# First attention: the norm's last step on ScalarE, top values copied once per four tiles, expert weights rounded once out of a ring of raw chunks

## The chip, the cores and the metric

The kernel runs on one core of one Trainium2 chip. The metric is the device time of one execution in microseconds (us), lower is better. The kernel before was timed three times; a further execution was profiled.

## What is computed

Two transformer layers over 16 sequences of 256 tokens of width 256, each a cross attention over 77 context rows followed by a mixture of experts. Cut to the part that the change touches, the first layer:

```python
x = x + _L0_xattn_ref(_layernorm(x), ctx, ctx, ...)   # 16 heads of 16, query and key layernorm, softmax
x = x + _L0_ffn_ref(_layernorm(x), moe_router, moe_w13, moe_w2)
# inside the second:
router_logits = jnp.einsum('td,de->te', x_flat, moe_router)          # 8 experts
topk_logits, topk_idx = jax.lax.top_k(router_logits, 2)
w13_out = jax.lax.ragged_dot(x_sort, moe_w13, group_sizes)           # 8 x 256 x 1024 weights
```

The first attention phase ends each tile of 128 tokens with x1 = x + attention, xn = layernorm(x1), the eight router logits, and their sorted values and indices. In its idle time it also splits the 8 MB of expert weights w13 into a rounded high part, which stays in SBUF, and a low part, which goes to DRAM and is loaded again by the next phase.

## The kernel before

The program is a row of phases (projection, first attention, first routing, first experts, second attention, and so on), each a block that all engines leave together at a barrier. Within a phase every engine runs its own instruction list in order and waits on semaphores.

The change lies in `attention0_phase`. It handles 32 tiles of 128 tokens (`NT`), each in two halves of eight heads, so 64 halves u (`NU`). The function `half(u)` is written once for each engine and says what that engine does in half u. A stage with skew T works in half u on the tile with 2t = u - T. In half u TensorE does the scores of u (L777), the transposes of the probabilities of u-1 (L788) and the products with V of u-2 (L805); in even halves it adds the transposes L814 and L823 and the router product (L841), in odd ones the output projection (L833, T_WP = 7) and the transpose of xn (L852, T_X = 9). VectorE takes the maximum (L665) and subtracts it (L670) for every half; in odd halves it normalises the heads, writes x1 (L699) and takes its mean and variance; in even halves it waits for POOL's inverse root, applies the norm (L159, `ln.apply`) and sorts the eight logits of the tile with skew T_R = 10 (`top_of`, L477 to L485). ScalarE evicts PSUM (L730, L742, L749, L756) and does the exponentials (L735). POOL runs two halves ahead (`LEAD`): it spreads queries and keys (L623, L630, L636), adds the bias (L649) and computes the inverse root (L108, L110). Halves 16 to 63 are a hardware loop of eight halves; halves 0 to 15 and the tail, halves 64 to 74, are written out.

The weights: SP loads w13 into SBUF in eight pieces of 1 MB near the phase's start. They are handled as 64 chunks of 128 x 256 (`CHUNKS`), one for each half from u = 8. ScalarE writes the rounded chunk to `low` (L723, T_HIGH), POOL subtracts it from the raw chunk (L640, T_LOW), and two halves after the first step ScalarE stores `low` (L760) and rounds the chunk in place (L762, T_ROUND). There are four `low` buffers.

SP's list for a tile s is: load x of tile s, store x1 of tile s-4 (L602), store xn of tile s-4 (L604). In the next phase SP loads `pad_row` (L1254) and the low weights (L1257).

Of the kernel before, what the change touches and what calls it, by code (L numbers as in the profile page):

```python
# [6 lines left out]
F32 = mybir.dt.float32  # L7
F32R = mybir.dt.float32r
# [8 lines left out]
P = 128  # L17
# [95 lines left out]
class LayerNorm:  # L113
# [30 lines left out]
    def shift(self, pool, t):  # L144

        p = t.mod(self.ring)
        pool.wait_ge(self.s_rstd, t.n + 1)
        pool.tensor_scalar(self.less[p][:, :], self.mv[p][:, 0:1], self.rstd[p][:, :], -1.0, ALU.mult, ALU.mult)\
            .then_inc(self.s_less, 1)
# [327 lines left out]
def top_of(dve, g, scores, top, ix, t, s_scores, s_top, s_ix, passed):  # L477

    wait_alone(dve, s_scores, t.n + 1, passed[0])
    dve.max(top[:, :], scores[:, :]).then_inc(s_top, 1)  # L480
    wait_alone(dve, s_top, t.n + 1, passed[0])
    dve.max_index(ix[:, :], top[:, :], scores[:, :]).then_inc(s_ix, 1)
    dve.tensor_copy(g.top_v[:, bass.ds(t.n * 8, 8)], top[:, :])
    wait_alone(dve, s_ix, t.n + 1, passed[0])
    dve.tensor_copy(g.top_i[:, bass.ds(t.n * 8, 8)], ix[:, :])  # L485


def attention0_phase(nc, g):
# [3 lines left out]
    with ctx:  # L492
        def sb(name, shape, dt=F32):
# [4 lines left out]
        NU = NT * NG  # L498
        VW = H * (DH + 1)
# [21 lines left out]
        top = [sb(f"top{i}", [P, 8]) for i in range(2)]  # L521
        ix = [sb(f"ix{i}", [P, 8], U32) for i in range(2)]
        low = [sb(f"low{i}", [P, CHUNK], F32R) for i in range(4)]
        s_w, s_next, s_w13_first, s_w13, w_high, w_low, w_round = (sem(n) for n in (
            "s_w", "s_next", "s_w13_first", "s_w13", "w_high", "w_low", "w_round"))
        s_x, x1_st, xn_st = ([sem(f"{n}{i}") for i in range(2)] for n in ("s_x", "x1_st", "xn_st"))
        low_st = [sem(f"low_st{i}") for i in range(4)]
# [15 lines left out]
        T_RAW, T_N, T_O, T_WP, T_X, T_R = 4, 5, 6, 7, 9, 10  # L543
# [8 lines left out]
        T_HIGH, T_LOW, T_ROUND = 8, 9 + LEAD, 10  # L552

        W13_LATE = 3
# [10 lines left out]
        def _(sp):  # L565
# [3 lines left out]
            for dst, src in ((g.tri, g.ins["tri"]), (g.iota, g.ins["iota"]), (g.iota16, g.ins["iota16"]),  # L569
                             (g.not_first, g.ins["not_first"][:, 0:E0 * NT]), (g.tokval, g.ins["tokval0"])):  # L570
                sp.dma_start(dst[:, :], src).then_inc(s_next, 16)
# [8 lines left out]
            def expert_weights(e):  # L580
                n = DC * 2 * M0
                sp.dma_start(g.w13[:, e * n:(e + 1) * n], g.ins["w13"][:, e * n:(e + 1) * n])\
                    .then_inc(s_w13 if e else s_w13_first, 16)

            expert_weights(0)
            for t in range(2):
                input_rows(At(None, 0, t))
            for e in range(1, E0 - W13_LATE):
                expert_weights(e)

            def tile(s):
                t = s
                if t.within(NT):
                    if not (t.loop is None and t.off < 2):
                        input_rows(t)
                    if t.loop is None and 2 <= t.off < 2 + W13_LATE:
                        expert_weights(E0 - W13_LATE + t.off - 2)
                t = s.shift(-4)
                if t.within(NT):
# [4 lines left out]
                    sp.dma_start(g.xn[bass.ds(t.n * P, P), :], xn[p][:, :]).then_inc(xn_st[p], 16)  # L604

            steps(sp, 6, NT, NT + 4, 2, tile)
# [4 lines left out]
            for st in low_st:  # L611
                sp.wait_ge(st, CHUNKS // 4 * 16)

        @block.gpsimd
        def _(pool):
            def half(u):
# [21 lines left out]
                if i is not None:  # L638
                    pool.wait_ge(w_high, i.n + 1)
                    pool.tensor_tensor(low[i.mod(4)][:, :], chunk(i), low[i.mod(4)][:, :], ALU.subtract).then_inc(w_low, 1)  # L640
# [10 lines left out]
                if t is not None:  # L651
                    ln.invert(pool, t)

# [3 lines left out]
        def _(dve):  # L657
            dve.memset(ps_raw, 0.0).then_inc(ps_clear, 1)

            def half(u):  # L660
# [42 lines left out]
                if t is not None:  # L703
# [3 lines left out]
                    top_of(dve, g, lg[p], top[p], ix[p], t, lg_done, m8_done, ix_done, passed)  # L707
# [4 lines left out]
        def _(act):  # L712
            def half(u):
                i = chunk_at(u, T_HIGH)
                if i is not None:
                    if i.loop is None and i.off == 0:
                        act.wait_ge(s_w13_first, 16)
                    if i.loop is None and i.off == CHUNKS // E0 - 1:

                        act.wait_ge(s_w13, (E0 - 1) * 16)  # L720
# [1664 lines left out]
```

## Time and profile before

| | us |
|---|---|
| median of 3 timed runs | 1511.56 (1511.35 to 1512.79) |
| the profiled execution's own time | 1501.55 |
| its span, first to last instruction | 1499.7 |
| first attention phase in it | 110.6 to 373.5 |

The profiled execution took 10.0 us less than the median of the timed ones, and 1.85 us of its time lie outside its span. Times of the trace are microseconds from the span's start. Mean granted TensorE clock is 0.938 of full.

### The profile page before, as it was taken

The numbers are of one execution on the slowest core, as the hardware profiler recorded it, in microseconds if no ns is written. First come the engines' busy times: TensorE is split into PE (matmuls) and PEld (weight loads), VectorE is DVE, ScalarE is ACT, GpSimd is POOL, SyncE is SP. The second block draws the span as 40 slices with busy tenths as digits, with TensorE's granted clock in tenths as the row PEclk, the third lists the DMA queues.
The fourth block names the chain that finished last, engine by engine and source line by source line (L and its number), as shares of the span: only waits on it lengthen the run. The fifth ranks groups of instructions, "written<-read, shape, count | busy, mean of one in ns | idle before, by whom it ended". The sixth has DMA issues, their size and how long they took to land. (4 is left out here: it accounts for less than half of the span.)

```text
span 1499.7 us, 29032 instructions
## 1 busy us (share of the span) xinstructions
PE 1334.3 (89%) x7717; PEld 1055.5 (70%) x7718; DVE 766.2 (51%) x1962; ACT 585.5 (39%) x1311; POOL 654.1 (44%) x903
## 2 busy tenths in 40 slices
PE   7989999997979999999994998569999998577877
PEld 4656777775668888888883776258888885366655
DVE  4875888886822233223224886913333333154546
ACT  2555777775322222222222775533333332111110
POOL 1213656564023333333332763055555551655552
PEclk9998999998989999999996998579999999888989
DMA  2208222223721111111115885455555575333433
GB/s 92 63 29 326 91 88 84 87 79 112 281 95 50 52 52 49 49 52 52 49 39 172 260 227 178 174 182 156 158 164 164 161 141 124 103 112 106 122 115 99
DMA packets 117292, 179.69 MB, mean 120 GB/s; under 512 B 17178, under 2 KB 91947, under 8 KB 113900
## 3 DMA queue, kind: packets, MB, share of 16 engines
q1 hardware_dynamic: 80980, 100.29, 20.1%
q0 software_dynamic: 20640, 56.39, 14.2%
q10 hardware_dynamic: 15608, 22.25, 4.2%
q8 instruction: 29, 0.48, 0.1%
q14 instruction: 35, 0.29, 0.1%
HBM read 115.00 MB, written 59.64 MB: 116 GB/s over the span
## 5 line engine op out<-in xcount | busy, mean ns | idle before, releaser
L1228 POOL DMA_INDIRECT xg<-t_xn,token x160 | 151.3, 946 | 160.8 <-remote 61.7
L2168 POOL DMA_INDIRECT su_yg<-t_y,slot x128 | 123.2, 963 | 114.3 <-DVE su_acc L2197 44.5
L2106 PE MATMUL psum<-gu,m_xT 128*128 x640 | 153.4, 383 | 3.2 <-ACT m_xT L2037 3.2
L1465 PE MATMUL psum<-w,m_hT 128*128 x568 | 134.5, 380 | 0.8 <-ACT m_hT L1384 0.8
L1403 DVE TENSOR_TENSOR m_h<-psum,m_h 128x512 f32<-128x512 f32 x71 | 49.2, 692 | 162.7 <-ACT m_h L1378 88.9
L2106 PEld LDWEIGHTS psum<-gu,m_xT 128*128 128x128 f32 x640 | 116.5, 192 | 16.5 <-issue 3.7
L1444 PE MATMUL psum<-w,m_xT_high 128*128 x284 | 119.2, 420 | 0.0
L1444 PE MATMUL psum<-w,m_xT_low 128*128 x284 | 113.3, 399 | 0.0
L1444 PE MATMUL psum<-w_low,m_xT_high 128*128 x284 | 112.6, 396 | 0.0
L1465 PEld LDWEIGHTS psum<-w,m_hT 128*128 128x128 f32 x568 | 102.4, 190 | 12.2 <-issue 1.2
L1378 ACT ACTIVATE m_h<-psum 128x512 f32<-128x512 f32 x71 | 42.4, 597 | 151.7 <-PE psum L1444 151.7
L2073 DVE COPY m_y<-psum 128x512 f32<-128x512 f32 x80 | 54.9, 687 | 79.0 <-remote 37.0
L2065 DVE TENSOR_TENSOR m_h<-psum,m_sg 128x256 f32<-128x256 f32 x80 | 34.0, 425 | 119.0 <-ACT m_sg L2044 60.1
L1858 ACT ACTIVATE sh_sg<-psum 128x512 f32<-128x512 f32 x32 | 19.1, 598 | 193.3 <-PE psum L1837 75.7
L2037 ACT ACTIVATE m_xT<-psum 128x512 f32<-128x512 f32 x80 | 47.8, 598 | 108.6 <-remote 87.7
L777 PE MATMUL psum<-at_kblk,at_q_s 128*128 128x308 f32 x256 | 82.9, 448 | 7.3 <-DVE w L670 4.0
L730 ACT ACTIVATE at_prT<-psum 77x1024 f32<-77x1024 f32 x64 | 65.3, 1020 | 59.8 <-PE psum L788 59.8
L1384 ACT ACTIVATE m_hT<-psum 128x512 f32<-128x512 f32 x71 | 42.5, 599 | 112.4 <-PE psum L1465 112.4
L2127 PE MATMUL psum<-dn,m_hT 128*128 x320 | 84.0, 388 | 1.8 <-DVE m_y L2073 1.7
L1352 POOL DMA_INDIRECT t_y<-top_v,dest x36 | 35.5, 986 | 108.8 <-DVE top_v L1410 108.5
L1219 POOL DMA_INDIRECT xg<-t_xn,token x54 | 52.5, 973 | 68.4 <-POOLq L1237 48.4
L1352 POOL DMA_INDIRECT t_y<-top_i,dest x35 | 34.5, 987 | 106.2 <-DVE top_i L1410 100.7
(305 smaller groups left out, 3185.6 us busy)
## 6 DMA issues: line engine op xcount, KB each, us to landing
t_y<-m_y SPq DMA_DIRECT2D x80, 256.0 KB
w<-in_w SPq DMA_DIRECT2D x8, 1024.0 KB, 11.1
t_x<-at_x SPq DMA_DIRECT2D x64, 128.0 KB, 2.0
t_w_low<-at_low ACTq DMA_DIRECT2D x64, 128.0 KB, 1.7
w_low<-t_w_low SPq DMA_DIRECT2D x8, 1024.0 KB, 13.1
at_yg<-t_y SPq DMA_DIRECT2D x32, 256.0 KB, 3.5
gu<-in_gu ACTq DMA_DIRECT2D x8, 1024.0 KB, 11.8
w<-in_x SPq DMA_DIRECT2D x16, 256.0 KB, 2.7
```

Source lines behind the costliest of these rows:

```text
L730: act.activation(prT[p][0:LK, :].rearrange("p (a k) -> p a k", a=2), ps_tp[0:LK, :, :], ACT.Copy)\
L777: last = pe.matmul(ps_s[:, a, 0:HW], q_s[p][:, gr * P:(gr + 1) * P], kblk[b.mod(2)][:, (2 * gr + a) * HW:(2 * gr + a + 1) * HW], start=Tru ...
L1219: pool.indirect_dma_start(out=g.xg0[j % GB][:, :], out_offset=None, in_=g.xn, in_offset=bass.IndirectOffsetOnAxis(ap=g.token[:, j:j + 1], ...
L1228: pool.indirect_dma_start(out=g.xg1[j % GB][:, k * D:(k + 1) * D], out_offset=None, in_=g.xn4, in_offset=bass.IndirectOffsetOnAxis(ap=g.to ...
L1352: pool.indirect_dma_start(out=g.y0, out_offset=bass.IndirectOffsetOnAxis(ap=g.dest[:, j:j + 1], axis=0), in_=y[p][:, :], in_offset=None).t ...
L1403: dve.tensor_tensor(h[p][:, :], ps_gu[p][:, 1, :], h[p][:, :], ALU.mult).then_inc(h_done, 1)
L1444: last = pe.matmul(ps_gu[p][:, half, :], x[p][:, tile], w[:, at], start=(c == 0 and w is w13_high and x is xT_high), stop=(c == DC - 1 and ...
L1465: last = pe.matmul(ps_y[:, 0:D], hT[:, c * P:(c + 1) * P], g.w2[:, bass.ds(ex * (MC * D) + c * D, D)], start=(c == 0), stop=(c == MC - 1))
L2073: dve.tensor_copy(y[p][:, :], ps_y[p][:, :]).then_inc(y_out, 1)
L2106: last = pe.matmul(ps_gu[p][:, k * 2 * M1:(k + 1) * 2 * M1], xT[p][:, at:at + P], g.gu[:, bass.ds(ex[k] * (DC * 2 * M1) + c * 2 * M1, 2 * ...
L2127: last = pe.matmul(ps_y[p][:, k * D:(k + 1) * D], hT[j.mod(HELD)][:, k * P:(k + 1) * P], g.dn[:, bass.ds(ex[k] * D, D)], start=True, stop= ...
L2168: pool.indirect_dma_start(out=yg[p][k][:, :], out_offset=None, in_=g.y1, in_offset=bass.IndirectOffsetOnAxis(ap=g.slot[:, at:at + 1], axis ...
```

## The change

1. The last step of the norm moves from VectorE (`ln.apply`, half 2t+8, before x1 and the sort) to ScalarE (`ln.apply_scalar`, T_XA = 8, the last instruction of the half). For it POOL computes one more column, minus mean times inverse root (`ln.shift`), right behind the inverse root.
2. The sorted values and indices of four tiles are gathered in one buffer each (`RANKED`), and copied to `top_v` and `top_i` once for four tiles instead of once for each tile.
3. The raw weights no longer go straight into SBUF's w13. SP loads them chunk by chunk, 128 KB each, into a ring of eight buffers (the eighth is the table `not_first`, which the phase does not use). ScalarE rounds a chunk once, from the ring into w13; POOL subtracts w13 from the ring's buffer in place; SP stores it. ScalarE's second rounding and its 64 stores are gone.
4. SP's list for a tile s becomes: store x1 and xn of tile s-4, load x of tile s-1, load raw chunks 2s-6 and 2s-5, store low chunks 2s-12 and 2s-11. At the phase's end SP waits for the last store out of `not_first` and then loads that table.

```diff
     def shift(self, pool, t):
 
         p = t.mod(self.ring)
-        pool.wait_ge(self.s_rstd, t.n + 1)
+        wait_alone(pool, self.s_rstd, t.n + 1, self.s_passed[1])
         pool.tensor_scalar(self.less[p][:, :], self.mv[p][:, 0:1], self.rstd[p][:, :], -1.0, ALU.mult, ALU.mult)\
             .then_inc(self.s_less, 1)
...
-def top_of(dve, g, scores, top, ix, t, s_scores, s_top, s_ix, passed):
+def top_of(dve, scores, top, ix, t, s_scores, s_top, s_ix, passed):
 
     wait_alone(dve, s_scores, t.n + 1, passed[0])
-    dve.max(top[:, :], scores[:, :]).then_inc(s_top, 1)
+    dve.max(top, scores[:, :]).then_inc(s_top, 1)
     wait_alone(dve, s_top, t.n + 1, passed[0])
-    dve.max_index(ix[:, :], top[:, :], scores[:, :]).then_inc(s_ix, 1)
-    dve.tensor_copy(g.top_v[:, bass.ds(t.n * 8, 8)], top[:, :])
-    wait_alone(dve, s_ix, t.n + 1, passed[0])
-    dve.tensor_copy(g.top_i[:, bass.ds(t.n * 8, 8)], ix[:, :])
...
-        low = [sb(f"low{i}", [P, CHUNK], F32R) for i in range(4)]
+        RING = 8
+        low = [sb(f"low{i}", [P, CHUNK], F32R) for i in range(RING - 1)] + [g.not_first[:, :].bitcast(F32R)]
+        low_st, s_raw = ([sem(f"{n}{i}") for i in range(RING)] for n in ("low_st", "s_raw"))
...
+            def weights(i):
+
+                p = i.mod(RING)
+                wait(sp, low_st[p], i.div(RING).n * 16)
+                sp.dma_start(low[p][:, :].bitcast(F32), g.ins["w13"][:, bass.ds(i.n * CHUNK, CHUNK)]).then_inc(s_raw[p], 16)
+
+            def weights_low(i):
+                p = i.mod(RING)
+                sp.wait_ge(w_low, i.n + 1)
+                sp.dma_start(g.w13_low_d[:, bass.ds(i.n * CHUNK, CHUNK)], low[p][:, :].bitcast(F32)).then_inc(low_st[p], 16)
+
             for t in range(2):
                 input_rows(At(None, 0, t))
-            for e in range(1, E0 - W13_LATE):
-                expert_weights(e)
+
+            W13_FROM, W13_LOW = 3, 6
...
             def tile(s):
-                t = s
-                if t.within(NT):
-                    if not (t.loop is None and t.off < 2):
-                        input_rows(t)
-                    if t.loop is None and 2 <= t.off < 2 + W13_LATE:
-                        expert_weights(E0 - W13_LATE + t.off - 2)
                 t = s.shift(-4)
                 if t.within(NT):
                     p = t.mod(2)
@@ -602,14 +596,27 @@
                     sp.dma_start(g.x1[bass.ds(t.n * P, P), :], x1[p][:, :]).then_inc(x1_st[p], 16)
                     sp.wait_ge(x_norm, t.n + 1)
                     sp.dma_start(g.xn[bass.ds(t.n * P, P), :], xn[p][:, :]).then_inc(xn_st[p], 16)
-
-            steps(sp, 6, NT, NT + 4, 2, tile)
+                t = s.shift(-1)
+                if t.within(NT) and not (t.loop is None and t.off < 2):
+                    input_rows(t)
+                t = s.shift(-W13_FROM)
+                if t.within(CHUNKS // 2):
+                    for i in range(2):
+                        weights(t.times(2).shift(i))
+                t = s.shift(-W13_LOW)
+                if t.within(CHUNKS // 2):
+                    for i in range(2):
+                        weights_low(t.times(2).shift(i))
+
+            steps(sp, 8, NT, NT + W13_LOW, 4, tile)
+            sp.wait_ge(low_st[RING - 1], CHUNKS // RING * 16)
+            sp.dma_start(g.not_first[:, :], g.ins["not_first"][:, 0:E0 * NT]).then_inc(s_next, 16)
...
                     pool.wait_ge(w_high, i.n + 1)
-                    pool.tensor_tensor(low[i.mod(4)][:, :], chunk(i), low[i.mod(4)][:, :], ALU.subtract).then_inc(w_low, 1)
+                    p = i.mod(RING)
+                    pool.tensor_tensor(low[p][:, :], low[p][:, :].bitcast(F32), chunk(i), ALU.subtract)\
+                        .then_inc(w_low, 1)
...
+                    ln.shift(pool, t)
...
-                t = tile_at(u, T_WP + 1)
-                if t is not None:
-                    p = t.mod(2)
-
-                    wait(dve, xn_st[p], t.div(2).n * 16)
-                    wait(dve, x_t, t.shift(-1).n)
-                    ln.apply(dve, x1[p][:, :], xn[p][:, :], t).then_inc(x_norm, 1)
...
-                    top_of(dve, g, lg[p], top[p], ix[p], t, lg_done, m8_done, ix_done, passed)
+                    at = slice(t.mod(RANKED) * 8, (t.mod(RANKED) + 1) * 8)
+                    top_of(dve, lg[p], top[:, at], ix[:, at], t, lg_done, m8_done, ix_done, passed)
+                    if t.mod(RANKED) == RANKED - 1:
+                        at = bass.ds(t.shift(1 - RANKED).n * 8, RANKED * 8)
+                        dve.tensor_copy(g.top_v[:, at], top[:, :])
+                        wait_alone(dve, ix_done, t.n + 1, passed[0])
+                        dve.tensor_copy(g.top_i[:, at], ix[:, :])
...
-                    wait(act, low_st[i.mod(4)], i.div(4).n * 16)
-                    act.activation(low[i.mod(4)][:, :], chunk(i), ACT.Copy).then_inc(w_high, 1)
+                    act.wait_ge(s_raw[i.mod(RING)], (i.div(RING).n + 1) * 16)
+                    act.activation(chunk(i).bitcast(F32R), low[i.mod(RING)][:, :].bitcast(F32), ACT.Copy).then_inc(w_high, 1)
...
-                i = chunk_at(u, T_ROUND)
-                if i is not None:
-                    act.wait_ge(w_low, i.n + 1)
-                    act.dma_start(g.w13_low_d[:, bass.ds(i.n * CHUNK, CHUNK)], low[i.mod(4)][:, :].bitcast(F32))\
-                        .then_inc(low_st[i.mod(4)], 16)
-                    act.activation(chunk(i).bitcast(F32R), chunk(i), ACT.Copy).then_inc(w_round, 1)
+                t = tile_at(u, T_XA)
+                if t is not None:
+                    p = t.mod(2)
+
+                    wait(act, xn_st[p], t.div(2).n * 16)
+                    wait(act, x_t, t.shift(-1).n)
+                    ln.apply_scalar(act, x1[p][:, :], xn[p][:, :], t).then_inc(x_norm, 1)
```

Two places show what this does to the order. The first is ScalarE's list in the tail, from half 64 on, after the loop. Before (`w` is w13, or scratch space in the spare of w2 in L742's case):

```order
L723 ACTIVATE at_low<-w 128x256
L730 ACTIVATE at_prT<-psum 77x1024
L749 ACTIVATE at_oT<-psum 128x256
L760 DMA t_w_low<-at_low 128x256
L762 ACTIVATE w<-w 128x256
L723 ACTIVATE at_low<-w 128x256
L742 ACTIVATE w<-psum 128x512
L756 ACTIVATE at_xnT<-psum 128x256
L760 DMA t_w_low<-at_low 128x256
L762 ACTIVATE w<-w 128x256
L723 ACTIVATE at_low<-w 128x256
L749 ACTIVATE at_oT<-psum 128x256
```

The same halves 64, 65 and the start of 66 of the changed kernel:

```order
L726 ACTIVATE w<-at_low 128x256
L733 ACTIVATE at_prT<-psum 77x1024
L752 ACTIVATE at_oT<-psum 128x256
L154 ACTIVATE at_xn<-at_x,at_ln_less,at_ln_rstd 128x256
L726 ACTIVATE w<-at_low 128x256
L745 ACTIVATE w<-psum 128x512
L759 ACTIVATE at_xnT<-psum 128x256
L726 ACTIVATE w<-at_low 128x256
L752 ACTIVATE at_oT<-psum 128x256
L154 ACTIVATE at_xn<-at_x,at_ln_less,at_ln_rstd 128x256
```

L760 and L762 are gone, the norm L154 stands last in each even half, and the first instruction of every half (L726) now reads a ring buffer that a DMA fills. The second place is SP's list at the end of the phase. Before, the stores of x1 and xn of the last three tiles and the branch out of the block:

```order
L602 DMA t_x<-at_x 128x256
L604 DMA t_xn<-at_xn 128x256
L602 DMA t_x<-at_x 128x256
L604 DMA t_xn<-at_xn 128x256
L602 DMA t_x<-at_x 128x256
L604 DMA t_xn<-at_xn 128x256
L492 UNCONDITIONAL_BRANCH
```

The same end in the changed kernel:

```order
L596 DMA t_x<-at_x 128x256
L598 DMA t_xn<-at_xn 128x256
L579 DMA at_low<-in_w 128x256
L579 DMA not_first<-in_w 128x256
L584 DMA t_w_low<-at_low 128x256 x2
L596 DMA t_x<-at_x 128x256
L598 DMA t_xn<-at_xn 128x256
L584 DMA t_w_low<-at_low 128x256 x5
L584 DMA t_w_low<-not_first 128x256
L613 DMA not_first<-in_not_first 128x256
```

Behind the last xn store stand six stores of low chunks, and the load of the table, which waits for the last of them.

## Rows read from the trace of the kernel before

**Rows 1.** Engine time in two stretches: PE, PEld, DVE, ACT, POOL busy, clock, DMA.

```profile
150.00:250.00 100.00, 100.00 (x968) 79.56 (x962) 86.55 (x215) 75.56 (x148) 63.98 (x104) 1.00 0.27 88
350.00:377.00 27.00, 17.65 (x123) 12.99 (x116) 16.93 (x65) 13.53 (x33) 10.89 (x19) 0.71 0.37 124
```

**Rows 2.** Timeline, TensorE: a half's first scores product, every eighth half; start, duration.

```profile
222.65 0.68 PE L777 MATMUL psum<-at_kblk,at_q_s 128*128 128x308 f32 x2
...
252.56 0.69 PE L777 MATMUL psum<-at_kblk,at_q_s 128*128 128x308 f32 x2
...
284.23 1.20 PE L777 MATMUL psum<-at_kblk,at_q_s 128*128 128x308 f32 x4
...
314.14 1.20 PE L777 MATMUL psum<-at_kblk,at_q_s 128*128 128x308 f32 x4
```

**Rows 3.** Timeline, VectorE and POOL, at the slow half and 30 us before.

```profile
227.62 0.16 DVE L485 COPY top_i<-at_ix 128x8 uint32 x1
...
257.54 0.40 POOL L636 COPY w<-kv 77x272 f32 x1
...
257.54 2.49 DVE L485 COPY top_i<-at_ix 128x8 uint32 x1
...
259.28 0.72 POOL L640 TENSOR_TENSOR at_low<-w,at_low 128x256 fp32r<-128x256 f32 x1
...
259.95 0.79 DVE L665 TENSOR_REDUCE at_mx<-psum 128x8 f32<-128x616 f32 x1
...
261.62 0.82 PEld L777 LDWEIGHTS psum<-at_kblk,at_q_s 128*128 128x128 f32 x4 [1.66 <-DVE w L670]
```

**Rows 4.** Groups by line inside the phase: busy us, mean ns of one | idle before.

```profile
L159 DVE TENSOR_SCALAR at_xn<-at_x,at_ln_mv,at_ln_rstd 128x256 f32<-128x256 f32 x27 | 26.2, 969 | 0.0
...
L762 ACT ACTIVATE w<-w (+1 forms) x64 | 26.6, 415 | 0.6 <-issue 0.2
...
L108 POOL TENSOR_SCALAR at_ln_rstd<-at_ln_mv 128x1 f32<-128x1 f32 x13 | 2.9, 221 | 36.7 <-DVE at_ln_mv L137 36.7
```

**Rows 5.** DMA issues by line, 150 to 350 us: KB each, median us to landing.

```profile
t_w_low<-at_low ACTq DMA_DIRECT2D x53, 128.0 KB, 1.7
at_x_in<-in_x SPq DMA_DIRECT2D x27, 128.0 KB, 2.1
```

**Rows 6.** Timeline, ScalarE in the steady part.

```profile
340.52 0.42 ACT L762 ACTIVATE w<-w  x1
...
344.42 0.38 ACT L756 ACTIVATE at_xnT<-psum 128x256 f32<-128x256 f32 x1
```

**Rows 7.** Timeline of the phase's end, all engines.

```profile
359.09 0.70 DVE L159 TENSOR_SCALAR at_xn<-at_x,at_ln_mv,at_ln_rstd 128x256 f32<-128x256 f32 x1 [1.21 <-POOL at_ln_rstd L110]
...
362.95 0.38 ACT L749 ACTIVATE at_oT<-psum 128x256 f32<-128x256 f32 x1 [1.38 <-PE psum L823]
...
363.42 2.05 PE L833 MATMUL psum<-at_wp,at_oT 128*128 128x256 f32 x4
...
366.22 0.42 DVE L699 TENSOR_TENSOR at_x<-psum,at_xb 128x256 f32<-128x256 f32 x1
...
368.65 0.70 DVE L159 TENSOR_SCALAR at_xn<-at_x,at_ln_mv,at_ln_rstd 128x256 f32<-128x256 f32 x1 [1.21 <-POOL at_ln_rstd L110]
...
369.37 0.33 SPq L604 DMA_DIRECT2D t_xn<-at_xn  x1
...
371.16 0.43 ACTq L760 DMA_DIRECT2D t_w_low<-at_low  x1
...
372.77 0.17 DVE L485 COPY top_i<-at_ix 128x8 uint32<-128x8 uint32 x1
...
373.47 0.35 SPq L1254 DMA_DIRECT2D r_pad_row<-in_pad_row  x1
...
373.87 4.12 SPq L1257 DMA_DIRECT2D w_low<-t_w_low  x8
```

More of the change, by code:

```diff
@@ L474, in _ @@
             steps(pe, FIRST, LAST, TOTAL, BODY, step)
-def top_of(dve, g, scores, top, ix, t, s_scores, s_top, s_ix, passed):
+def top_of(dve, scores, top, ix, t, s_scores, s_top, s_ix, passed):
     wait_alone(dve, s_scores, t.n + 1, passed[0])
-    dve.max(top[:, :], scores[:, :]).then_inc(s_top, 1)
+    dve.max(top, scores[:, :]).then_inc(s_top, 1)
     wait_alone(dve, s_top, t.n + 1, passed[0])
-    dve.max_index(ix[:, :], top[:, :], scores[:, :]).then_inc(s_ix, 1)
-    dve.tensor_copy(g.top_v[:, bass.ds(t.n * 8, 8)], top[:, :])
-    wait_alone(dve, s_ix, t.n + 1, passed[0])
-    dve.tensor_copy(g.top_i[:, bass.ds(t.n * 8, 8)], ix[:, :])
+    dve.max_index(ix, top, scores[:, :]).then_inc(s_ix, 1)
 def attention0_phase(nc, g):
@@ L498, in attention0_phase @@
         NU = NT * NG
+        RANKED = 4
         VW = H * (DH + 1)
@@ L520, in attention0_phase @@
         lg = [sb(f"lg{i}", [P, E0]) for i in range(2)]
-        top = [sb(f"top{i}", [P, 8]) for i in range(2)]
-        ix = [sb(f"ix{i}", [P, 8], U32) for i in range(2)]
-        low = [sb(f"low{i}", [P, CHUNK], F32R) for i in range(4)]
-        s_w, s_next, s_w13_first, s_w13, w_high, w_low, w_round = (sem(n) for n in (
-            "s_w", "s_next", "s_w13_first", "s_w13", "w_high", "w_low", "w_round"))
+        top, ix = sb("top", [P, RANKED * 8]), sb("ix", [P, RANKED * 8], U32)
+        RING = 8
+        low = [sb(f"low{i}", [P, CHUNK], F32R) for i in range(RING - 1)] + [g.not_first[:, :].bitcast(F32R)]
+        s_w, s_next, w_high, w_low = (sem(n) for n in ("s_w", "s_next", "w_high", "w_low"))
         s_x, x1_st, xn_st = ([sem(f"{n}{i}") for i in range(2)] for n in ("s_x", "x1_st", "xn_st"))
-        low_st = [sem(f"low_st{i}") for i in range(4)]
+        low_st, s_raw = ([sem(f"{n}{i}") for i in range(RING)] for n in ("low_st", "s_raw"))
         v_ready = sem("v_ready")
@@ L541, in attention0_phase @@
         block = ctx.enter_context(nc.Block())
-        T_RAW, T_N, T_O, T_WP, T_X, T_R = 4, 5, 6, 7, 9, 10
+        T_RAW, T_N, T_O, T_WP, T_XA, T_X, T_R = 4, 5, 6, 7, 8, 9, 10
         FIRST, BODY, TOTAL = 16, 8, NU + T_R + 1
@@ L550, in tile_at @@
             return s.div(2) if s.mod(2) == 0 and s.within(NU) else None
-        T_HIGH, T_LOW, T_ROUND = 8, 9 + LEAD, 10
-        W13_LATE = 3
+        T_HIGH, T_LOW = 8, 9 + LEAD
         def chunk_at(u, skew):
@@ L569, in _ @@
             for dst, src in ((g.tri, g.ins["tri"]), (g.iota, g.ins["iota"]), (g.iota16, g.ins["iota16"]),
-                             (g.not_first, g.ins["not_first"][:, 0:E0 * NT]), (g.tokval, g.ins["tokval0"])):
+                             (g.tokval, g.ins["tokval0"])):
                 sp.dma_start(dst[:, :], src).then_inc(s_next, 16)
@@ L611, in _ @@
             for st in low_st:
-                sp.wait_ge(st, CHUNKS // 4 * 16)
+                sp.wait_ge(st, CHUNKS // RING * 16)
         @block.gpsimd
@@ L715, in half @@
                 if i is not None:
[L716 to L720, printed above, removed]
-                    wait(act, low_st[i.mod(4)], i.div(4).n * 16)
-                    act.activation(low[i.mod(4)][:, :], chunk(i), ACT.Copy).then_inc(w_high, 1)
+                    act.wait_ge(s_raw[i.mod(RING)], (i.div(RING).n + 1) * 16)
+                    act.activation(chunk(i).bitcast(F32R), low[i.mod(RING)][:, :].bitcast(F32), ACT.Copy).then_inc(w_high, 1)
                 v = u.shift(-1)
```

5 lines of the change are left out of this document (removed).

## The prediction

> **What bounds the kernel now.** I first asked for the engines' busy time in stretches of the first attention phase [rows 1]. The columns are the stretch, its length, then busy time of matmuls, weight loads, VectorE, ScalarE and POOL, the clock, the DMA share and GB/s. In the steady part TensorE is busy all of 100 us, VectorE 86.6, ScalarE 75.6, POOL 64.0. A busy matmul row alone does not prove a bound, so I looked for a rhythm. The first scores product of a half, taken every eighth half, starts at 222.65, 252.56, 284.23 and 314.14 [rows 2]. The distances are 29.91, 31.67 and 29.91 us: eight halves cost 29.91 us, or 3.74 each, and one stretch of eight costs 1.76 more. Such a constant step, beside VectorE work whose instructions vary in length, says that TensorE's own list sets the pace, and VectorE only where it falls far behind.
>
> The one slow half shows how far [rows 3]. VectorE's copy of the indices (L485) starts at 257.54, at the very time at which POOL starts L636, and lasts 2.49 us, to 260.03. POOL's last instruction of that unbroken run, L640, ends at 259.28 + 0.72 = 260.00. The maximum of the next half starts only then, and TensorE's weight load for the scores finds nothing to do for 1.66 us. The same copy 30 us earlier took 0.16 us. So the copy lost a race for something it shares with POOL, and it waited for the whole run of POOL's instructions.
>
> The third stretch is the tail, from 350 us on: TensorE is busy 17.7 of 27 us, the clock is at 0.71 in the mean, and chains of small steps over all engines decide [rows 1, 7].
>
> **The change, part by part.**
>
> *VectorE loses the norm.* 969 ns for each tile, 26.2 us over 27 tiles [rows 4]. Since TensorE is the bound, this is worth nothing in the steady part. What it could free is the slack that the 2.49 us copy used up. It also loses three of four pairs of copies; those in a slow half are what matters. The remaining pair comes for tile t with t mod 4 = 3, in halves with u mod 8 = 0. The slow half was 38 (counting the maxima), that is u mod 8 = 6, and a long POOL run with the key spreading is there in every half with u mod 4 = 2. So the remaining copies fall outside of it. I take the whole 1.76 us as gain: **-1.76**. Bounds: 0, if a remaining copy meets such a run, and -1.76, for there was one.
>
> The Trainium skill (SBUF — State Buffer, Who interferes with whom) says that such a VectorE copy and a POOL instruction take a port pair as an exclusive lock for one whole instruction, and the loser blocks. By that rule the copy would have waited 0.40 us for L636, TensorE would have lost nothing, and the term would be 0. The row shows a wait through four instructions, and the sum goes by the row.
>
> *ScalarE.* It loses 64 roundings of 415 ns [rows 4] and 64 DMA issues, and gains 32 norms over the same 128 x 256 elements; I take 0.41 us from L762, its nearest row. Two thirds of a rounding's room are left over; the norm takes the place of L762 at 340.52 in the even half [rows 6]. Cost in the steady part 0, hidden by TensorE.
>
> *POOL* gains a one column instruction for each tile, 0.22 us as L108 [rows 4], about 0.35 with its wait. POOL is at 64% and, with work for two halves ahead, has the room. 0 in the steady part, 0.35 in the tail's last tile.
>
> *The raw chunks.* The first instruction of each ScalarE half now waits for a DMA. SP issues it behind the xn store of tile s-4, which waits for the new norm in half 2s; the chunk is wanted in half 2s+2. In the steady part: norm ends 341.03 (in L762's place, 340.52, with the time of L749 before it unchanged), 0.25 us for the semaphore, then the xn store, the x load and the first chunk load at about 0.45 each, so issue at 342.2, landing 2.1 us later [rows 5] at 344.3. ScalarE is free for it after L756, 344.42 + 0.38 = 344.80 [rows 6]. Half a microsecond is left, and behind it nearly a microsecond before the next eviction and about one more before TensorE misses the exponentials. So 0 here. The DMA traffic near the phase's start gets lighter (8 MB are no longer fetched at once), but nothing on the path waits for it.
>
> *In the tail* the halves are short on work and the room is gone. Before, tile 29's norm started at 359.09 and ended 359.79, ScalarE evicted tile 31's heads (L749) at 362.95, and the projection L833 started at 363.42 at the low clock level (2.05 us) [rows 7]. Now norm 29 ends at about 360.0 (POOL's extra column, ScalarE 0.41 instead of VectorE 0.70), the xn store and the load of chunk 60 are issued at 360.3 and 360.6, and the chunk lands at 362.7. ScalarE's rounding of it stands ahead of L749: 362.9 to 363.3, L749 to 363.65, L833 from 363.85, 0.4 later than before. It ends at 365.9, so x1 of tile 31 starts at 366.2, as before (366.22). VectorE would have been ready long before, since it no longer waits for POOL and has no norm: its gain in the tail is given back to the chunk's DMA. From x1 to the norm's start were 2.43 us (366.22 to 368.65); with 0.45 more for the column and ScalarE 0.41 the norm of tile 31 ends at 366.2 + 2.43 + 0.45 + 0.41 = 369.5. VectorE's end after it would be some 0.4 us later than 372.94 was.
>
> *SP's end* is what counts. Before, the last low chunk was stored by ScalarE at 371.16 and landed 1.7 us later, at 372.9, when VectorE's last copy ended also (372.77 + 0.17); the next phase began at 373.47 [rows 5, 7]. Now SP issues the xn store at 369.7 and behind it six stores. Eight issues in a row took 4.12 us, 0.515 each [rows 7], so the sixth store starts at 369.7 + 0.38 + 5 x 0.515 = 372.65 and lands at 374.35. Only then is the table's load issued, 0.2 us later; it lands after 2.1 us [rows 5] at 376.65. With the 0.4 to 0.5 us of the barrier the next phase begins at about 377.1: **+3.6**. Bounds: -0.4 if the DMA chain overlapped better than I read it and VectorE's end, earlier by the unhindered norm, decided; +5.5 if each of the two DMAs takes a microsecond more.
>
> *The sum:* -1.76 + 3.6 = +1.84 us. Against the profiled execution's own 1501.55 us that is 1503.4. It is 0.12% of the time, and I carry it over to the median unchanged: 1511.56 + 1.84 = **1513.4 us**. A measurement of this kernel can tell about 0.2%, 3.0 us, from no change, so the forecast is no change that can be told.
>
> **The rivals.**
>
> *More copies lose the race in the timed runs (faster).* The timed runs took 10.0 us more than the profiled one. If that were such stalls, there would be 10.0 / 1.76 = 5.7 more of them; sixteen tiles have the copy near POOL's long run. The change would remove them all: 1511.56 - 10.0 - 1.76 + 3.6 = 1503.4. For it speaks that the race of rows 3 was decided within 0.01 us. Against it, that the three runs lie within 1.4 us, and that the rest of the difference may be clock or launch. It is faster by over 3.0 us from three more stalls on.
>
> *The tail does not grow (no change, or barely faster).* If SP's last store lands while VectorE still sorts, only the table's load, or nothing, is added: 1511.56 - 1.76 - 0.4 = 1509.4 up to 1511.6. It stays within 0.2%.
>
> *A chunk that comes late in the steady part (slower).* The place is ScalarE's first instruction in each even half. TensorE starts to wait when a chunk lands more than 2.1 + 0.5 + 0.95 + 0.9 = about 4.5 us after its issue. Seven transfers of 128 KB for each tile are now in one queue, where two queues shared five. Each 0.5 us beyond that point would be paid in some 26 tiles: 13 us, or 1511.56 + 1.84 + 13 = 1526.4. The median of 2.1 us speaks against it.
>
> *The tail grows more (slower).* If both last DMAs take the upper bound, +5.5 - 1.76 = 3.7: 1515.3.
>
> *The change does nothing:* with the one stall returning somewhere else, +3.6: 1515.2, also just over 0.2%.
>
> **How the numbers follow.** My forecast with its own spread (1509.5 to 1514.5) and the rival of a tail that doesn't grow are both within 0.2%: 0.45 and 0.10. More stalls in the timed runs: 0.22. Late chunks 0.10; a tail over 5 us or a stall elsewhere 0.13. So faster 0.22, same 0.55, slower 0.23. The range leaves out about one in ten on each side: below, the greater part of the stall case reaches to 1505.5; above, it takes in the long tail and the mildest late chunks, to 1517.
>
> **What would show it.** Right: the steps of eight halves all at 29.91 us; L726 never waits for a DMA in the loop, but does in halves 66 and 68 of the tail; six low stores in a row behind the last xn store, and the next phase's first instruction about 4 us after VectorE's last copy (0.5 before). Wrong: a step of eight halves below 29.9 would mean that TensorE was not the bound; waits of L726 in the loop that show on TensorE; a copy of 128 x 32 of over 2 us; or later phases that change with an unchanged instruction list, as by the clock.

## The result and the profile after

The changed kernel took 1515.19 us in the median of 20 timed runs, the kernel before 1511.02 us beside it (20 runs; the three known ahead gave 1511.56). The ratio is 1.0032, with a 95% interval of 1.0016 to 1.0048: slower by 2.4 to 7.3 us. The forecast was 1513.4 us and "no change that can be told". The time fell inside the range and 1.8 us from the forecast. But 4.2 us are more than the 3.0 us (0.2%) that the forecast took as its limit, and the interval excludes 1, so by that limit the outcome is "slower". One run of the changed kernel (4607.62 us) and one each of E3, E4 and E8 below (1519.06, 2270.01 and 5546.67 us) count as slow runs, which stand in the medians but not in the ratios.

The profiled execution of the changed kernel took 1512.32 us, 10.8 us more than that of before. Most of that difference is not the change. The timed runs of the kernel before lie 15 to 22 us apart in each comparison, and the profile of before was among its shortest. So whole times are compared by timed runs only, and what the change does is read where it acts, between three marks that every trace has: TensorE's first weight load for the scores (the phase's start), its last such group (half 63, end of the steady part), and SP's `pad_row` load (the next phase's start). In the changed kernel these are, from the timelines of weight loads and of SP:

```profile
113.79 0.50 PEld L781 LDWEIGHTS psum<-at_kblk,at_q_s 128*128 128x128 f32 x2 [3.23 <-POOL at_kblk L637]
...
346.58 0.82 PEld L781 LDWEIGHTS psum<-at_kblk,at_q_s 128*128 128x128 f32 x4
...
375.81 0.34 SPq L1258 DMA_DIRECT2D r_pad_row<-in_pad_row  x1
```

Before, the same marks stood at 112.26, 347.67 and 373.47. So the part up to half 63 went from 235.41 to 232.79 us, and the tail from 25.80 to 29.23. The phase grew by 0.81 us. Of the first part's 2.62 us, 1.74 are the lost slow half (halves 11 to 63 took 196.18 and now 194.44). The other 0.88 lie in the third half of the phase, which took 3.97 us before and 3.09 now; that comes and goes with the clock. The granted clock was 0.50 from 120 to 122 us before, and 1.00 throughout the same half of the changed kernel. The three profiles of the kernel before (the first, and E9 and E12 below) have 3.97, 3.09 and 3.94 us there.

The steady rhythm is TensorE's, as [rows 2]. The matmul timeline of the changed kernel shows two of its steps, read at the second of a half's four products:

```profile
219.82 0.94 PE L781 MATMUL psum<-at_kblk,at_q_s 128*128 128x308 f32 x3
...
249.73 0.94 PE L781 MATMUL psum<-at_kblk,at_q_s 128*128 128x308 f32 x3
...
279.65 0.94 PE L781 MATMUL psum<-at_kblk,at_q_s 128*128 128x308 f32 x3
```

29.91 and 29.92 us for eight halves, with no slow one. VectorE's load fell and TensorE's pace did not move. The engines' time from 150 to 350 us says it once more (columns as in [rows 1]; before, VectorE had 173.51 us here and ScalarE 149.09):

```profile
150.00:350.00 200.00, 200.00 (x1935) 159.03 (x1934) 146.48 (x360) 146.40 (x267) 129.46 (x227) 1.00 0.38 120
```

VectorE gave up 27 us of work. ScalarE came out nearly even, since its norm costs more than I took. The groups by line in the same stretch:

```profile
L726 ACT ACTIVATE w<-at_low 128x256 f32 (+1 forms) x46 | 18.9, 411 | 3.0 <-DMA at_low<-in_w 2.2
L154 ACT ACTIVATE at_xn<-at_x,at_ln_less,at_ln_rstd 128x256 f32<-128x256 f32 x27 | 16.0, 591 | 0.0
```

The norm takes 591 ns, a plain copy of the same shape 411. The first row shows also that the raw chunks are nearly late in the loop: five waits of over 0.15 us, 2.2 us in all and 0.80 the longest, one before the loop and four in it. None of them reaches TensorE, which waits for no other engine in this stretch.

The tail is where the time went. ScalarE's timeline there:

```profile
357.82 0.42 ACT L726 ACTIVATE w<-at_low 128x256 fp32r<-128x256 f32 x1 [2.26 <-DMA at_low<-in_w]
358.14 0.37 ACT L752 ACTIVATE at_oT<-psum 128x256 f32<-128x256 f32 x1
...
362.01 0.42 ACT L726 ACTIVATE w<-at_low 128x256 fp32r<-128x256 f32 x1 [1.69 <-DMA at_low<-in_w]
362.34 0.36 ACT L752 ACTIVATE at_oT<-psum 128x256 f32<-128x256 f32 x1
...
367.17 0.60 ACT L154 ACTIVATE at_xn<-at_x,at_ln_less,at_ln_rstd 128x256 f32<-128x256 f32 x1 [0.94 <-POOL at_ln_less L148]
```

In halves 66 and 68 ScalarE waits 2.26 and 1.69 us for a raw chunk (0.72 more in half 70), and the eviction L752, on which TensorE's projection depends, stands behind it. SP's timeline at the end, which answers to the lower part of [rows 7]:

```profile
367.79 0.33 SPq L598 DMA_DIRECT2D t_xn<-at_xn  x1
368.17 2.42 SPq L584 DMA_DIRECT2D t_w_low<-at_low  x5
370.63 0.45 SPq L584 DMA_DIRECT2D t_w_low<-not_first  x1
372.48 0.34 SPq L613 DMA_DIRECT2D not_first<-in_not_first  x1
375.81 0.34 SPq L1258 DMA_DIRECT2D r_pad_row<-in_pad_row  x1
```

Six stores, a wait until the last has landed, the table's load, a wait for that, and the barrier. VectorE's last copy had ended at 371.23, so 4.6 us before the next phase; before it was 0.5.

### The profile page after: what moved, and what is told of

Read it like the earlier page. It is cut to its first block and busy times, and to the rows that moved or that the text cites. A ratio compares the mean times of both kernels' runs of the same rounds, so it can differ in the third digit from the quotient of the medians.

```text
span 1510.5 us, 29130 instructions
## 1 busy us (share of the span) xinstructions
PE 1329.5 (88%) x7717; PEld 1051.3 (70%) x7718; DVE 736.4 (49%) x1882; ACT 582.8 (39%) x1279; POOL 661.9 (44%) x935
```

## The experiments

Each profile is read by the same marks. "Halves 11 to 63" is taken between TensorE's weight loads of these two halves. The columns for the whole time compare timed runs with those of the kernel before on the same chip. The ratio is estimated from the single runs and is not the quotient of the two medians: for E2 that would be 1.0047, for E3 1.0018.

| kernel | halves 11 to 63 | tail | phase | median / before beside it | ratio (95%) |
|---|---|---|---|---|---|
| before | 196.18 | 25.80 | 261.21 | | |
| changed | 194.44 | 29.23 | 262.02 | 1515.19 / 1511.02 | 1.0032 (1.0016 to 1.0048) |
| E1 ring alone | 196.20 | 29.83 | 264.38 | 1510.55 / 1505.66 | 1.0023 (0.9988 to 1.0057) |
| E2 norm alone | 200.70 | 23.43 | 263.09 | 1512.78 / 1505.66 | 1.0063 (1.0031 to 1.0094) |
| E3 copies alone | 194.44 | 24.86 | 257.65 | 1508.44 / 1505.66 | 0.9998 (0.9967 to 1.0028) |
| E4 before, table late | 194.44 | 28.32 | 261.87 | 1509.28 / 1505.66 | 1.0014 (0.9984 to 1.0044) |
| E5 table first | 194.44 | 27.17 | 259.96 | 1508.19 / 1506.44 | 1.0022 (0.9998 to 1.0045) |
| E6 chunks ahead | 194.44 | 26.46 | 259.82 | 1508.77 / 1506.44 | 1.0018 (0.9995 to 1.0042) |
| E7 E5 and E6 | 194.44 | 23.62 | 256.41 | 1507.51 / 1506.44 | 1.0007 (0.9978 to 1.0036) |
| E8 changed, again | 194.44 | 29.12 | 261.91 | 1510.02 / 1508.52 | 1.0020 (1.0000 to 1.0041) |
| E9 before, again | 194.44 | 25.80 | 258.58 | 1502.17 / 1508.52 | 0.9969 (0.9946 to 0.9993) |
| E10 E7, norm on VectorE | 194.44 | 25.24 | 258.73 | 1506.95 / 1508.52 | 0.9991 (0.9966 to 1.0016) |
| E11 E7, again | 194.43 | 23.66 | 257.37 | 1506.33 / 1505.56 | 1.0012 (0.9987 to 1.0037) |
| E12 before, third | 194.44 | 25.80 | 259.43 | 1505.48 / 1505.56 | 1.0005 (0.9980 to 1.0030) |

**E1: the ring alone.** Items 3 and 4 of the change; the norm stays on VectorE, the copies stay one for each tile. Against the changed kernel:

```diff
+                t = tile_at(u, T_WP + 1)
...
+                    ln.apply(dve, x1[p][:, :], xn[p][:, :], t).then_inc(x_norm, 1)
...
+                    top_of(dve, g, lg[p], top[p], ix[p], t, lg_done, m8_done, ix_done, passed)
...
-                t = tile_at(u, T_XA)
...
-                    ln.apply_scalar(act, x1[p][:, :], xn[p][:, :], t).then_inc(x_norm, 1)
```

> Only the ring of raw chunks with SP's loads and stores; norm and top copies as before. Theory A (the cost is SP's list at the phase's end, and the raw chunk that ScalarE waits for in the tail): the tail, from TensorE's last first-of-half weight load of the scores to SP's pad_row load, is 28.5 to 30 us (before 25.80, after 29.23), the steady part is 29.91 us per eight halves, and the time is 2 to 4 us longer than before's. Rival B (the cost came with the norm on ScalarE): the tail is within 0.7 us of 25.8 and the time within noise of before's.

The tail is 29.83 us, 4.0 more than before. The ring alone carries the tail's whole cost. By the ratio the kernel is 3.5 us slower, as expected, though the interval holds 1. The steady part, which I had expected at 29.91 for every eight halves, had the slow half again, in the same place. The timelines of VectorE, POOL and TensorE's weight loads there:

```profile
256.61 2.49 DVE L485 COPY top_i<-at_ix 128x8 uint32 x1
...
256.61 0.40 POOL L647 COPY w<-kv 77x272 f32 x1
...
260.69 0.82 PEld L778 LDWEIGHTS psum<-at_kblk,at_q_s 128*128 128x128 f32 x4 [1.66 <-DVE w L683]
```

**E2: the norm alone**, item 1 only, last in ScalarE's half behind the second rounding, which stays, as do the four low buffers and ScalarE's stores. Against the kernel before:

```diff
-                t = tile_at(u, T_WP + 1)
...
-                    ln.apply(dve, x1[p][:, :], xn[p][:, :], t).then_inc(x_norm, 1)
...
+                t = tile_at(u, T_WP + 1)
...
+                    ln.apply_scalar(act, x1[p][:, :], xn[p][:, :], t).then_inc(x_norm, 1)
```

> Only the norm on ScalarE (with POOL's extra column); four low buffers, ScalarE's second rounding and stores as before. Theory A: the tail stays at 25.8 us within 1, steady part 29.91 per eight halves, the time within 2 us of before's; a slow half by a lost copy can still appear. Rival B: the tail grows by 2 us or more, and the time by as much.

Both expectations missed. The tail is not 25.8 but 23.43, and the steady part is 6.3 us longer than an undisturbed one. The kernel is slower by 0.63% (0.31 to 0.94), 4.7 to 14.2 us; its phase is longer than that of E9 and E12 (the kernel before, below) by 4.5 and 3.7 us, which accounts for the lower end of that.

In fourteen places of the steady part a half took 3.80 to 3.97 us instead of at most 3.76, some 2.1 us in all. Twelve of them lie four halves apart: they are the halves in which VectorE's copies meet POOL's spreading of the keys. The timelines of VectorE, POOL and TensorE's weight loads at one of them:

```profile
198.03 1.08 DVE L485 COPY top_i<-at_ix 128x8 uint32 x1
...
196.68 2.40 POOL L630 TENSOR_TENSOR at_kblk<-kv,hmask 128x616 f32<-128x616 f32 x2
...
199.84 0.80 DVE L671 TENSOR_TENSOR w<-psum,at_mx 128x616 f32<-128x616 f32 x1
...
200.70 0.82 PEld L778 LDWEIGHTS psum<-at_kblk,at_q_s 128*128 128x128 f32 x4 [0.18 <-DVE w L671]
```

The copy ends when POOL's spreading ends (196.68 + 2.40 = 199.08). Without the norm ahead of it VectorE's sort comes earlier, and its copies fall under that instruction. VectorE's subtraction L671 is then late, and TensorE waits for it. ScalarE is also short of room: before its next eviction it is idle for 0.49 us in the mean (23.0 us over 47 waits), where the changed kernel has 0.94 (49.6 us over 53). But no wait of TensorE for ScalarE is recorded in this stretch. The other 4.1 us are two halves in a row of 6.23 and 5.39 us, behind a value copy of 1.23 us and an index copy of 2.49 right after each other on VectorE. So item 1 by itself costs time in the steady part, and what the trace shows of it are copies that wait for POOL. The changed kernel has a quarter of these copies, through item 2, and in other halves: its value copy took 0.60 to 0.72 us in six of them, and TensorE never waited. No run separates whether ScalarE's second rounding has a share in E2's loss.

**E3: the copies alone**, item 2, against the kernel before.

```diff
-                    top_of(dve, g, lg[p], top[p], ix[p], t, lg_done, m8_done, ix_done, passed)
...
+                    top_of(dve, lg[p], top[:, at], ix[:, at], t, lg_done, m8_done, ix_done, passed)
+                    if t.mod(RANKED) == RANKED - 1:
...
+                        dve.tensor_copy(g.top_v[:, at], top[:, :])
...
+                        dve.tensor_copy(g.top_i[:, at], ix[:, :])
```

> Only the sorted values and indices copied once per four tiles. If the 1.76 us stall before was one of several per timed run, the time drops by 2 us or more; if it is a rare event, the time is before's within noise (2 us) and the tail is 25.8 within 0.7 us. No copy of over 2 us in either case.

No slow half, a tail of 24.86 us (0.24 outside of what I gave it), and a whole time that can't be told from before's: 0.9998. The interval's lower end, 0.9967, is 5.0 us, so a saving of the 5.7 stalls of 1.76 us that the rival asked for is excluded; one or two stalls for each timed run are not.

**E4: the kernel before with only the table's load moved to the end.**

```diff
-                             (g.not_first, g.ins["not_first"][:, 0:E0 * NT]), (g.tokval, g.ins["tokval0"])):
+                             (g.tokval, g.ins["tokval0"])):
...
             steps(sp, 6, NT, NT + 4, 2, tile)
+            sp.wait_ge(low_st[3], CHUNKS // 4 * 16)
+            sp.dma_start(g.not_first[:, :], g.ins["not_first"][:, 0:E0 * NT]).then_inc(s_next, 16)
```

> The kernel before, with the load of not_first alone moved to the phase's end, behind the landing of the last low chunk. Theory A: SP's pad_row load comes 2.1 to 2.6 us later, so the tail is 28.0 to 28.5 us, and the time is about 2.3 us (0.15%) longer. Rival: the barrier already waits on something else, and the tail stays at 25.8.

The tail grew by 2.52 us, as theory A has it. SP's timeline:

```profile
371.15 0.35 SPq L608 DMA_DIRECT2D not_first<-in_not_first  x1
...
374.15 0.35 SPq L1256 DMA_DIRECT2D r_pad_row<-in_pad_row  x1
```

From the load's issue to the next phase 3.0 us. This run has every instruction of the loop as before, and no slow half.

**E5: the table as the ring's first buffer**, so that the last low chunk in it is chunk 56 and not chunk 63, and its load ahead of the last xn store.

```diff
-        low = [sb(...) for i in range(RING - 1)] + [g.not_first[:, :].bitcast(F32R)]
+        low = [sb(...) for i in range(RING - 1)]
+        low = [g.not_first[:, :].bitcast(F32R)] + low
...
+                    if s.loop is None and s.off == NT + 3:
+                        sp.wait_ge(low_st[0], CHUNKS // RING * 16)
+                        sp.dma_start(g.not_first[:, :], ...)
                     sp.wait_ge(x_norm, t.n + 1)
...
-            sp.wait_ge(low_st[RING - 1], CHUNKS // RING * 16)
-            sp.dma_start(g.not_first[:, :], ...)
```

> The changed kernel, with the table not_first as the ring's first buffer instead of its last, so that it is free two tiles earlier, and its load ahead of the last xn store. Theory A (two separate costs in the tail: the table's load behind the last store, and the late raw chunks): the tail falls by the load's 2.3 to 2.9 us, from 29.23 to between 26.3 and 27.0 us; ScalarE's waits for raw chunks stay at about 2.3, 1.7 and 0.7 us. Rival (the stores alone fill the queue and the load was hidden behind them): the tail stays above 28.5.

The tail is 27.17 us, 2.06 less than the changed kernel's, slightly short of the 2.3 expected. ScalarE's waits for chunks stayed (2.48, 1.40 and 0.42 us). SP's timeline, with the load out of the chain:

```profile
365.31 0.34 SPq L600 DMA_DIRECT2D not_first<-in_not_first  x1
366.76 0.33 SPq L602 DMA_DIRECT2D t_xn<-at_xn  x1
367.13 2.90 SPq L585 DMA_DIRECT2D t_w_low<-at_low  x6
372.20 0.34 SPq L1260 DMA_DIRECT2D r_pad_row<-in_pad_row  x1
```

**E6: raw loads and low stores ahead of SP's wait for xn.**

```diff
                     sp.dma_start(g.x1[bass.ds(t.n * P, P), :], x1[p][:, :]).then_inc(x1_st[p], 16)
-                    sp.wait_ge(x_norm, t.n + 1)
-                    sp.dma_start(g.xn[bass.ds(t.n * P, P), :], xn[p][:, :]).then_inc(xn_st[p], 16)
-                t = s.shift(-1)
-                if t.within(NT) and not (t.loop is None and t.off < 2):
-                    input_rows(t)
                 t = s.shift(-W13_FROM)
...
                         weights_low(t.times(2).shift(i))
+                t = s.shift(-4)
+                if t.within(NT):
+                    p = t.mod(2)
+                    sp.wait_ge(x_norm, t.n + 1)
+                    sp.dma_start(g.xn[bass.ds(t.n * P, P), :], xn[p][:, :]).then_inc(xn_st[p], 16)
+                t = s.shift(-1)
+                if t.within(NT) and not (t.loop is None and t.off < 2):
+                    input_rows(t)
```

> The changed kernel, with SP's loads of raw chunks and stores of low chunks put ahead of its wait for xn, the table's load still last. Theory A: ScalarE's waits for raw chunks in the tail are gone (under 0.3 us each), two stores fewer stand behind the last xn store, and the tail falls to between 26 and 27.5 us; the steady part stays at 29.91 per eight halves. Rival (the raw chunk was not what held ScalarE): only the two stores count, 1.0 us, and the tail is 28 us or more.

As theory A has it: 26.46 us, and no wait of ScalarE for a chunk in the tail. The waits of ScalarE from 346 us on are now for POOL's column and for TensorE:

```profile
ACT at_xn L154 <- POOL at_ln_less L148: 3.6, 3, 1.4
ACT at_xnT L762 <- PE psum L859: 1.5, 4, 0.5
```

The same view of the changed kernel:

```profile
ACT w L726 <- DMA at_low<-in_w: 4.7, 3, 2.3
ACT at_xnT L759 <- PE psum L856: 2.2, 4, 1.2
```

**E7: both.**

> Both mendings. Theory A: the costs add, the tail is 23 to 24.5 us, less than before's 25.8, because ScalarE's norm no longer holds VectorE up there; the phase from the first scores to the next phase is 256 to 258 us (before 261.2 with one stall and 259.4 without, after 262.0), and the time is 1 to 4 us shorter than before's. Rival: something else comes up behind them (POOL's subtractions), and the tail stays above 25 us.

The tail is 23.62 us, 5.61 less than the changed kernel's; E5 and E6 alone took off 2.06 and 2.77. The savings add, with 0.8 to spare. The tail is also 2.2 us shorter than before's 25.80: with the ring's two costs gone, the norm on ScalarE and the fewer copies do shorten it. SP's timeline:

```profile
365.79 0.33 SPq L613 DMA_DIRECT2D t_xn<-at_xn  x1
366.17 1.91 SPq L585 DMA_DIRECT2D t_w_low<-at_low  x4
370.24 0.34 SPq L1263 DMA_DIRECT2D r_pad_row<-in_pad_row  x1
```

Within the phase this kernel beats both: 256.41 us. In the whole time it does not show: 1.0007 (0.9978 to 1.0036), where I had expected it 1 to 4 us below before's.

**E8 and E9: the changed kernel and the kernel before once more,** unaltered.

> The changed kernel once more, unaltered. Theory A (the change acts in the first attention phase alone): steady part 194.4 us with no slow half, tail 29.0 to 29.5 us, phase 262 us; the rest of the span, from the next phase on, between 1126 and 1141 us like every other kernel's, no matter which. Rival C (the change also makes later phases longer): the rest is again longer than that of the kernel before run beside it by 3 us or more.

> The kernel before once more, unaltered, to see how often its slow half comes and how long the rest of its span is when profiled again. Theory A: tail 25.8 us within 0.3; steady part 194.4 or 196.2 us, as one copy wins or loses its race; the rest of the span 1130 to 1141 us, well above the 1126.2 of the first profile, which was one of the fastest runs. Rival C: the rest is again below 1129 us.

The marks repeat to 0.1 us: tails of 29.12 and 25.80. E9 has no slow half. The same copy and the same POOL instruction in E9, to be held against E1's above and [rows 3]:

```profile
256.57 0.17 DVE L485 COPY top_i<-at_ix 128x8 uint32 x1
...
256.58 0.43 POOL L636 COPY w<-kv 77x272 f32 x1
...
258.96 0.82 PEld L777 LDWEIGHTS psum<-at_kblk,at_q_s 128*128 128x128 f32 x4
```

Here the copy took 0.17 us; in E1 and in the first profile, at the same place, it took 2.49. The printed starts do not tell the two cases apart. In E12 (below) both stand at the same hundredth, as in E1, and the copy is short:

```profile
257.43 0.17 DVE L485 COPY top_i<-at_ix 128x8 uint32 x1
...
257.43 0.43 POOL L636 COPY w<-kv 77x272 f32 x1
```

The rows ahead of the meeting, in the first profile, say why the two start together:

```profile
257.23 0.39 DVE L483 COPY top_v<-at_top 128x8 f32 x1
...
256.33 1.26 POOL L630 TENSOR_TENSOR at_kblk<-kv,hmask 128x616 f32<-128x616 f32 x1
```

VectorE's value copy took 0.39 us instead of 0.17 and ended at 257.62, when POOL's spreading had ended (257.59). Both engines go on from there, within the same hundredth. This happens in every fourth half, thirteen times in the steady part of each profile of the kernel before.

From the next phase to the span's end ("the rest") E8 took 1500.1 - 374.20 = 1125.9 us and E9 1498.1 - 370.75 = 1127.35; the first two profiles had 1134.7 (changed) and 1126.2 (before). For E9 I had said 1130 to 1141, and under 1129 for rival C: there the rival's mark came true, and it did in E12 too (1128.1). Against rival C stands E8, the changed kernel with the shortest rest of all. Of the eleven profiles that are not of the kernel before, nine have 1130.4 to 1140.6 us, and only E8 and E11 (1126.7) less. So the rest alone does not settle it. Where the difference lies says more. From `pad_row` to the first instruction of the second attention phase, which takes in the first routing and the first experts, all fourteen profiles took 428.2 to 429.3 us (before 428.9 to 429.3, changed 429.1 and 429.2). The spread arises later, and with identical kernels: the last phase, to the span's end, took 245.3 us in E7 and 230.4 in E11. E9's whole time was 0.31% below that of the same program beside it, with an interval that excludes 1.

**E10: E7 with the norm back on VectorE.**

> Both mendings of the tail, with the norm back on VectorE and POOL's extra column gone; top copies per four tiles and the ring stay. If the norm on ScalarE is what made the tail shorter than before's, the tail grows from 23.62 to between 24.5 and 26 us (copies per four tiles alone had 24.86); if the norm's place is worth nothing, the tail stays within 0.5 us of 23.6. Steady part 194.4 us either way.

The tail is 25.24 us, 1.62 more than E7's, inside the first expectation. That is what the norm on ScalarE is worth, and only in the tail.

**E11 and E12: E7 and the kernel before once more.**

> The twice mended kernel once more, unaltered. Theory A: phase from first scores to next phase 256.4 us within 1, that is 2.2 us less than an undisturbed before (258.6) and 5.5 less than the changed kernel (261.9); the whole time differs from before's by less than the comparison can tell (ratio 0.996 to 1.001). Rival: the whole time is again above before's by over 0.1%, which would speak for a cost of the change outside of this phase.

> The kernel before a third time, unaltered, beside its own timed runs: what the comparison shows when nothing is changed. If the last such ratio, 0.9969 (0.9946 to 0.9993), was chance or the load of that program, this one lies anywhere between 0.996 and 1.004. Tail 25.8 us; steady part 194.4 or 196.2 us.

E11's phase is 257.37 us, its ramp 0.9 us longer than E7's with the clock; its ratio of 1.0012 lies 0.0002 over what I had given it and just past the 0.1% that I had named for the rival, a cost outside of this phase. Its interval (0.9987 to 1.0037) holds 1, but not the gain of 2.2 us (0.9985) that its phase would give. E12 gives 1.0005 with nothing changed. E9 and E12 together say that a ratio of 0.3% can come from loading the same program again.

## Why the forecast came out as it did

**TensorE is the bound of the steady part: right.** Halves 11 to 63 took 194.43 or 194.44 us in eleven of fourteen profiles, with VectorE's work in this stretch changed by 27 us. Taking the norm off VectorE was worth nothing there.

**The stall of 1.76 us: right in mechanism, wrong as a term.** I took the whole of it as gain, "for there was one". Of the five profiles that keep the copy for each tile and the norm on VectorE (before, E1, E4, E9, E12), two have it, both at the same place. In each of the five the index copy and POOL's instruction start within 0.01 us of each other thirteen times: 65 meetings, of which the copy lost two. The eight profiles with a copy for four tiles have no such stall. So what the change saves is about 2/5 of 1.75, or 0.7 us for a run, with five profiles as all there is for the share. This is the step that failed: the saving was sized at its full height where it should have been an expectation over runs. With 0.7 in place of 1.76 the sum is +2.9 and the forecast 1514.5. The rival with 5.7 more stalls in the timed runs fell with E3.

**ScalarE and POOL in the steady part at no cost: right together, though mis-sized.** The norm took 0.59 us instead of 0.41. Alone it does cost: E2 lost 2.1 us over fourteen halves and 4.1 in a long stall, both behind VectorE copies that waited for POOL. I had not seen that the sort moves under POOL's long instruction once the norm ahead of it is gone; in the changed kernel, with item 2, it does not show. (By its own rows ScalarE had a whole rounding's room left in each tile, 0.42 us, not two thirds of one.) POOL's column took 265 ns with 0.21 us of wait ahead of it, where I had 0.35 in all.

**The raw chunks in the loop: right in cost, wrong in the sign to look for.** I had said that ScalarE never waits for one in the loop, with half a microsecond of room and a landing time of 2.1 (the norm's end in that sum should read 340.93 by its rows, not 341.03); the loads took 2.4 in the median and ScalarE waited 2.2 us in all. TensorE lost nothing.

**The tail: right, +3.43 measured for +3.6, though two misses cancel in it.** The tail began 1.09 us earlier than before's (346.58 for 347.67), and that is taken off in what follows. The eviction behind the late chunk came at 362.34 (I said about 363.3; 0.1 later). Then I was too slow: the projection behind it took 1.50 us and not 2.05, for the granted clock was 0.67 in the mean from 362 to 366 us, where before's stood at 0.50 from 362.5 to 366.5. So x1 of tile 31 started at 364.29 (366.2; 0.8 earlier) and the sixth store at 370.63 (372.65; 0.9 earlier):

```profile
362.75 1.50 PE L837 MATMUL psum<-at_wp,at_oT 128*128 128x256 f32 x4 [1.70 <-ACT at_oT L752]
...
364.29 0.42 DVE L702 TENSOR_TENSOR at_x<-psum,at_xb 128x256 f32<-128x256 f32 x1 [2.32 <-PE psum L837]
```

Behind the stores I was too fast: from the table's load to the next phase it took 3.33 us, where I had 2.55. The next phase began at 375.81 (377.1; 0.2 earlier). E5 and E6 take the two costs away one by one, and E4 puts one of them into the kernel before. E7 shows that +3.4 is a net sum: the ring's order costs 5.6 us, and the norm and the copies give back 2.2, where I had the gain in the tail at nothing.

**The sign.** Outside the ramp, an undisturbed before takes 194.44 + 25.80 = 220.24 us and the changed kernel 223.67, so +3.4; over runs with the stall's share +2.7. The timed medians say +4.2, with 2.4 to 7.3 us as interval. The phase accounts for the lower part of that; E9 shows that the rest can be chance of the measurement. I found nothing outside the phase that the change made longer, and the two phases behind it are unchanged within 1.1 us. But E7 and E11, whose phase is shorter than before's, are not faster as a whole either. Whether there is a cost of a few us in later phases stays open. The range's upper side and the chance of 0.23 for slower held this outcome; as the likeliest one I had a change that cannot be told.

## What to carry to other kernels

When an engine with slack is relieved, look for what the relief costs at the phase's end. In a loop of 7.5 us for each tile seven transfers in one queue were free; in the tail, where a tile takes 4 us, a load issued behind the previous tile's last result, and a reload chained behind the last store, cost 5.6 us, of which 3.4 were left after what the norm and the copies gave. Order a DMA queue so that loads stand ahead of waits for results, and let a borrowed buffer be the one that is free first. And a stall seen in one profile is an event with a chance: profile the same kernel again before booking its removal.

## What the runs showed of the hardware

A VectorE copy of 128x8 that starts within 0.01 us of a POOL instruction took 0.17 us nearly always (63 of 65 times in five profiles), and 2.49 us the other two; then it waited through four POOL instructions, until POOL's run of back-to-back work ended. It did so once each in three different kernels (before, E1, E2), always 2.49 us. The Trainium skill (SBUF — State Buffer, Who interferes with whom) lets the loser wait for one whole instruction of the winner, here 0.40 us; the traces show the whole run.

A ScalarE activation of 128x256 from SBUF to SBUF took 411 ns as a plain copy and 591 ns with a bias and a scale for each partition.

The kernel before, loaded again and timed against itself, gave 0.9969 (0.9946 to 0.9993) once and 1.0005 (0.9980 to 1.0030) once.
